# Small operations of two layer normalisations on GpSimd instead of VectorE and ScalarE, in a two-layer graph kernel

## The reference

```python
# layer 0
h = max(layernorm(x), 0)
x = x + (A @ (h @ W0 + b0)) / deg[:, None]        # A = adj != 0, deg = column sums of A
# layer 1: attention with 4 heads of 512 columns
h = max(layernorm(x), 0)
ht = (h @ W1) by head; src = ht . a_src; dst = ht . a_dst
e = leaky_relu(src[:, None] + dst[None, :], 0.01) + adj
x = x + mean over heads of softmax(e) @ ht
```

## Time and profile before

| | us |
|---|---|
| median of 3 runs | 2461.21 |
| the profiled execution's own time | 2460.44 |
| its span | 2458.6 |
| PE busy | 2434.6 |
| DVE busy | 1873.5 |
| ACT busy | 1269.3 |
| POOL busy | 47.9 |

### The profile page before, as it was taken

One profiled execution on the slowest core, in us unless ns is written; L12 is line 12 of the kernel. 1 busy time (PEld: TensorE's weight loads), 2 busy tenths in 40 slices (PEclk: granted clock), 3 DMA queues, 4 the chain that ended last, 5 costly groups with the idle time before them and its releaser, 6 DMA issues.

```text
span 2458.6 us, 43025 instructions
## 1 busy us (share of the span) xinstructions
PE 2434.6 (99%) x12447; PEld 1182.6 (48%) x12447; DVE 1873.5 (76%) x2580; ACT 1269.3 (52%) x1886; POOL 47.9 (2%) x44
## 2 busy tenths in 40 slices
PE   7999999999999999999999999999999999999999
PEld 4444445444444444444444444444444444444787
DVE  7788787977778667886668866688766887767786
ACT  5645558644455444554445544455444554454554
POOL 0000000000000000000000000000000000000000
PEclk9999999999999999999999999999999999999999
DMA  4386756100221001210012100121001300001000
GB/s 150 105 269 187 257 185 227 35 2 3 60 64 39 0 5 51 73 39 0 5 43 81 39 0 5 38 86 35 4 5 34 90 34 3 2 13 49 27 1 10
DMA packets 74225, 144.76 MB, mean 59 GB/s; under 512 B 4489, under 2 KB 11915, under 8 KB 72970
## 3 DMA queue, kind: packets, MB, share of 16 engines
q1 hardware_dynamic: 74122, 143.61, 18.3%
HBM read 129.11 MB, written 13.70 MB: 58 GB/s over the span
## 4 chain that ended last, share of the span: by engine, by line
PE 82%; DVE 0%; ACT 0%; issue 0%; DVEq 0%; ACTq 0%
PE z_ps L798 71%; PE o_ps L826 11%; PE c_ps L812 0%; DVE t_reg L685 0%; DVE e_reg L496 0%; ACT t_reg L581 0%; DVE hl_reg L657 0%; ACT hl_reg L596 0%; DVE ao_reg L729 0%; ACT ring_reg L1568 0%; DVE z_reg L701 0%; ACT z_reg L608 0%; ACT ao_reg L1563 0%; DVE vv L1357 0%; DVE ao_reg L672 0%
## 5 line engine op out<-in xcount | busy, mean ns | idle before, releaser
L798 PE MATMUL z_ps<-hl_reg,h_reg 128*128 (+2 forms) x8712 | 1752.0, 364 | 1.3 <-DVE hl_reg L657 1.3
L798 PEld LDWEIGHTS z_ps<-hl_reg,h_reg 128*128 (+1 forms) x8712 | 852.4, 98 | 897.5 <-issue 2.3
L596 ACT ACTIVATE hl_reg<-t_reg (+2 forms) x363 | 360.7, 994 | 722.7 <-DVE t_reg L685 379.4
L657 DVE TENSOR_TENSOR hl_reg<-t_reg,hl_reg (+2 forms) x363 | 416.1, 1146 | 229.9 <-ACT hl_reg L596 228.0
L581 ACT ACTIVATE t_reg<-ring_reg,vv 128x512 f32 (+3 forms) x726 | 524.8, 770 | 66.0 <-DVE ao_reg L672 60.1
L685 DVE SCALAR_TENSOR_TENSOR t_reg<-t_reg,vv,e_reg (+3 forms) x728 | 509.9, 741 | 7.9 <-issue 7.9
L672 DVE TENSOR_TENSOR ao_reg<-ao_reg,t_reg 128x1024 f32<-128x1024 f32 (+1 forms) x336 | 383.4, 1141 | 0.0
L826 PE MATMUL o_ps<-w_reg,z_reg 128*128 128x512 f16 x1248 | 278.2, 379 | 0.9 <-DVE z_reg L701 0.9
L701 DVE SCALAR_TENSOR_TENSOR z_reg<-z_ps,z_reg 128x512 f16<-128x512 f32 (+1 forms) x112 | 73.1, 653 | 151.6 <-ACT z_reg L608 151.6
L826 PEld LDWEIGHTS o_ps<-w_reg,z_reg 128*128 128x128 f16 x1248 | 119.8, 98 | 140.9 <-DVE z_reg L701 1.2
L485 ACT ACTIVATE e_reg<-e_reg (+2 forms) x91 | 90.5, 995 | 152.5 <-DVE e_reg L496 152.5
(11 more groups left out here) (203 smaller groups left out, 1071.8 us busy)
## 6 DMA issues: line engine op xcount, KB each, us to landing
ring_reg<-adjT_in SPq DMA_DIRECT2D x78, 512.0 KB, 4.7
e_reg<-adjT_in SPq DMA_DIRECT2D x78, 512.0 KB, 3.7
ao_reg<-x_dram SPq DMA_DIRECT2D x6, 1024.0 KB, 5.5
out_dram<-ao_reg SPq DMA_DIRECT2D x6, 1024.0 KB, 4.6
ring_reg<-c_dram SPq DMA_DIRECT2D x23, 256.0 KB, 3.4
h_reg<-x_in SPq DMA_DIRECT2D x3, 1536.0 KB, 16.5
ring_reg<-x_in SPq DMA_DIRECT2D x9, 512.0 KB, 4.2
x_dram<-ring_reg SPq DMA_DIRECT2D x9, 512.0 KB, 5.1
```

The source lines that it names most:

```text
L596: nc.scalar.activation(hl_ring[:, g % HL_RING, 0, :, 0:W], t_ring[:, g % T_RING, :, 0:W], ACT.Copy).then_inc(hi_ready, 1)
L657: nc.vector.tensor_tensor(hl_ring[:, g % HL_RING, 1, :, 0:W], t_ring[:, g % T_RING, :, 0:W], hl_ring[:, g % HL_RING, 0, :, 0:W], ALU.subtr ...
L798: mm = nc.tensor.matmul(z_ps[:, k, 0:W], hk[hs], hl_ring[:, r, ps, u, 0:W], start=first and u == 0 and n == 0, stop=last and u == 1 and n ...
```

## The change

- Layer 0's tiles are grouped in nine groups instead of six: (0,2), (2,4), (4,6), (6,8), (8,10), (10,12), (12,16), (16,20), (20,26). The first tile of x comes in a transfer of its own, then the second; W0's tiles and b0 are loaded ahead of tiles 2 and 3.
- The square root (ACT) and the five scalar operations (DVE) go, for both normalisations. POOL makes `rs` and `nb` by eight operations: variance plus eps, the power minus one half, a Newton step in four, and the negated mean and the bias. POOL's first reduction L1001 now stands after layer 0's nine groups, and layer 1's nine groups stand between L1003 and L1005.
- PE issues `wake_clock` matmuls in the opening (60, 10, 16, 8, of 128 columns), multiplies tiles 0 and 1 by weight tile in the order in which the splits come, and uses four PSUM banks for projected tiles. DVE and ACT take their opening work in a new order.
- `MAX_DVE` is two steps earlier.
- `exp_e(0, 1)` on ACT moves behind `t1(0, 0, 0)`.
- At the end, the last head's product waits for `z_lo` tile by tile; the last tile is made, added and stored by halves of 256 columns, the 15-row part from ACT's queue.

The core of the diff:

```diff
         def ln_variances(dve, t0, t1, written, n_written, count):
             dve.wait_ge(written, n_written)
             for t in range(t0, t1):
                 nc.vector.bn_aggr(mv3[:, t], bst3[:, t]).then_inc(count, 1)
-            dve.wait_ge(count, n_count)
-            nc.vector.tensor_scalar(ve[:, t0:t1], mv3[:, t0:t1, 1], EPS, None, ALU.add).then_inc(s_var, 1)

+        def ln_scalars(pool, t0, t1, count, n_count):
+            c = slice(t0, t1)
+            pool.wait_ge(count, n_count)
+            pool_link(pool, nc.gpsimd.tensor_scalar(ve[:, c], mv3[:, c, 1], EPS, None, ALU.add))
+            pool_link(pool, nc.gpsimd.tensor_tensor(y0[:, c], ve[:, c], mhalf[:, c], ALU.pow))
+            pool_link(pool, nc.gpsimd.tensor_tensor(y1[:, c], y0[:, c], y0[:, c], ALU.mult))
+            pool_link(pool, nc.gpsimd.tensor_tensor(y1[:, c], y1[:, c], ve[:, c], ALU.mult))
+            pool_link(pool, nc.gpsimd.tensor_scalar(y1[:, c], y1[:, c], -0.5 * HS, 1.5 * HS, ALU.mult, ALU.add))
+            nc.gpsimd.tensor_scalar(ve[:, c], mv3[:, c, 0], -1.0, None, ALU.mult).then_inc(pool_step, 1)
+            pool_steps[0] += 1
+            pool_link(pool, nc.gpsimd.tensor_tensor(rs[:, c], y1[:, c], y0[:, c], ALU.mult))
+            nc.gpsimd.tensor_tensor(nb[:, c], ve[:, c], rs[:, c], ALU.mult).then_inc(s_ln, 1)
...
-        MAX_DVE = MAX_PE + A_RING + A_MORE + 2
+        MAX_DVE = MAX_PE + A_RING + A_MORE
...
             t1(0, 0, 0)
+            exp_e(act, 0, 1)
...
+                    if final:
+                        for c in range(it + 1):
+                            cols = slice(c * D // (it + 1), (c + 1) * D // (it + 1))
+                            for k in range(KT):
+                                if it == 0:
+                                    pe.wait_ge(z_lo, q * KT + k + 1)
+                                for m, (zs, ws) in enumerate(((0, 0), (0, 1), (1, 0))):
+                                    mm = nc.tensor.matmul(o_ps[:, it + c, cols], z16[:, zs, k, it * P:(it + 1) * P],
...
                 pool.wait_ge(s_const, 6)
+                pool_link(pool, nc.gpsimd.memset(mhalf[:], -0.5))
+                for t0, t1 in groups0:
+                    ln_scalars(pool, t0, t1, s_mv, t1)
                 nc.gpsimd.partition_all_reduce(warm[:], ones32[:], P, RMAX).then_inc(s_lib, 1)
                 pool.wait_ge(s_wmx, 2)
                 nc.gpsimd.partition_all_reduce(wmax[:], wmx1[:], P, RMAX).then_inc(s_wmax, 1)
+                pool.wait_ge(h0_relu, NT)
+                for c, (t0, t1) in enumerate(groups1):
+                    ln_scalars(pool, t0, t1, s_mv1, tiles_of(c + 1))
                 pool.wait_ge(s_dmx, 1)
                 nc.gpsimd.partition_all_reduce(dall[:], dmx[:], P, RMAX).then_inc(s_dall, 1)
...
+                def first_products():
+                    for k in range(KT):
+                        pe.wait_ge(s_w0hi, k + 1)
+                        for t in range(2):
+                            pe.wait_ge(ht_hi, t + 1)
+                            nc.tensor.matmul(hid_bank(t), ht0[:, t, 0, k], w0_16[:, 0, k], start=k == 0, stop=False)
+                    for t in range(2):
+                        pe.wait_ge(ht_lo, t + 1)
+                        for k in range(KT):
+                            nc.tensor.matmul(hid_bank(t), ht0[:, t, 1, k], w0_16[:, 0, k], start=False, stop=False)
+                    for k in range(KT):
+                        pe.wait_ge(s_w0lo, k + 1)
+                        for t in range(2):
+                            nc.tensor.matmul(hid_bank(t), ht0[:, t, 0, k], w0_16[:, 1, k], start=False, stop=False)
+
+                def wake_clock(n):
+                    for i in range(n):
+                        nc.tensor.matmul(z_ps[:, 1, 0:P], b0_one, b0_one, start=True, stop=True)

                 pe.wait_ge(s_const, 6)
+                wake_clock(60)
                 transpose0(0)
                 transpose0(1)
+                wake_clock(10)
                 pe.wait_ge(s_w0mx, 1)
                 nc.tensor.matmul(z_ps[:, 0, 0:1], ones_m, w0mx[:], start=True, stop=True).then_inc(w0b_ps, 1)
-                hidden(0)
+                wake_clock(16)
+                first_products()
                 transpose0(2)
-                hidden(1)
                 transpose0(3)
+                pe.wait_ge(s_b0lo, 1)
+                hidden_bias(0)
+                hidden_bias(1)
+                wake_clock(8)
+                hidden(2)
+                hidden(3)
+                transpose0(4)
+                transpose0(5)
```

More of the change, by code:

```diff
@@ L228, in ln_variances @@
                 nc.vector.bn_aggr(mv3[:, t], bst3[:, t]).then_inc(count, 1)
-            dve.wait_ge(count, n_count)
-            nc.vector.tensor_scalar(ve[:, t0:t1], mv3[:, t0:t1, 1], EPS, None, ALU.add).then_inc(s_var, 1)
-        def ln_scalars(dve, t0, t1, group):
+        def ln_scalars(pool, t0, t1, count, n_count):
             c = slice(t0, t1)
[L235 to L247, removed]
+            pool.wait_ge(count, n_count)
[5 more added lines that the diff above has]
+            nc.gpsimd.tensor_scalar(ve[:, c], mv3[:, c, 0], -1.0, None, ALU.mult).then_inc(pool_step, 1)
+            pool_steps[0] += 1
+            pool_link(pool, nc.gpsimd.tensor_tensor(rs[:, c], y1[:, c], y0[:, c], ALU.mult))
+            nc.gpsimd.tensor_tensor(nb[:, c], ve[:, c], rs[:, c], ALU.mult).then_inc(s_ln, 1)
         order = [FULL] + list(range(FULL))
@@ L649, in layer2_scalar @@
             blocks(act, body, first=1)
+            r1 = FULL * BW + P
+            for c in range(2):
+                cols = slice(c * D // 2, (c + 1) * D // 2)
+                act.wait_ge(o_out, FULL * H * IT + H * LASTW // P + 2 + c)
+                nc.scalar.dma_start(out[r1 + LAST16:N, cols], out_acc[LAST16:LASTP, 1, cols]).then_inc(rest_st, 16)
+            act.wait_ge(rest_st, 32)
         def layer2_vector(dve, split1_one):
@@ L728, in add_out @@
                         dve.wait_ge(o_out, f - n + 3)
+                    if isinstance(b, int) and b == FULL and h == H - 1 and it == n - 1:
+                        for c in range(2):
+                            cols = slice(c * D // 2, (c + 1) * D // 2)
+                            dve.wait_ge(o_done, f + 2 + c)
+                            nc.vector.scalar_tensor_tensor(out=out_acc[:, it, cols], in0=o_ps[:, it + c, cols],
+                                                           scalar=rcoef[:, it:it + 1], in1=out_acc[:, it, cols],
+                                                           op0=ALU.mult, op1=ALU.add).then_inc(o_out, 1)
+                        continue
                     nc.vector.scalar_tensor_tensor(out=out_acc[:, it], in0=o_ps[:, it % 3],
@@ L819, in project @@
                 q = b * H + h
-                pe.wait_ge(z_lo, (q + 1) * KT)
+                final = isinstance(b, int) and b == FULL and h == H - 1
+                if not final:
+                    pe.wait_ge(z_lo, (q + 1) * KT)
                 for it in range(n):
                     pe.wait_ge(o_out, o_before(b, h) + 2 + (it >= 3))
+                    if final:
[6 more added lines that the diff above has]
+                                    mm = nc.tensor.matmul(o_ps[:, it + c, cols], z16[:, zs, k, it * P:(it + 1) * P],
+                                                          w16[:, k, h, ws, cols], start=k == 0 and m == 0,
+                                                          stop=k == KT - 1 and m == 2)
+                            mm.then_inc(o_done, 1)
+                        if it == 0:
+                            row_sums(b, h)
+                        continue
                     for k in range(KT):
@@ L1136, in hidden_sum @@
                     h = hid32[:, t % 3]
-                    ins = nc.vector.scalar_tensor_tensor(out=h, in0=o_ps[:, 2] if t % 2 == 0 else c_ps[:], scalar=SH,
+                    ins = nc.vector.scalar_tensor_tensor(out=h, in0=hid_bank(t), scalar=SH,
                                                          in1=b0_bc, op0=ALU.mult, op1=ALU.add)
@@ L1183, in _ @@
                 transposed_lo(1)
-                for k in range(KT):
+                stats0(2)
+                stats0(3)
+                variances0(1)
+                w0_lo(0)
+                for k in range(1, KT):
                     w0_lo(k)
                 b0_lo()
+                transposed_lo(2)
+                stats0(4)
+                transposed_lo(3)
+                stats0(5)
+                variances0(2)
+                hidden_lo(0)
+                stats0(6)
+                hidden_lo(1)
+                stats0(7)
+                variances0(3)
+                transposed_lo(4)
+                transposed_lo(5)
                 dve.wait_ge(s_const, 6)
-                for i in range(2, NT + 6):
-                    if 2 <= i - 2 < NT:
+                for i in range(6, NT + 6):
+                    if 6 <= i - 2 < NT:
                         transposed_lo(i - 2)
```

(2 more changed lines are left out.)

143 lines of the change are left out of this document (67 added, 76 removed).

## The result

The changed kernel takes **2466.82 us** (median of 16 runs, 2465.97 to 2467.45) against 2461.20 for the kernel before on the same chip (2460.15 to 2463.80): ratio 1.0021, 95% interval 1.0015 to 1.0027. The forecast was 2468.3, range 2457.5 to 2477.5. The profiled execution spans 2464.7 us; before it was 2458.6, so 6.1 us are to be found. Hidden(4) is the projection of tile 4 (`hidden`), a link one of the eight small operations with the wait behind it, and the chain all eight.

What follows compares the result with a forecast made beforehand. PE is busy 99%; only the opening, the passage from layer 1 to layer 2 and the tail are latency-bound. Terms -1.3 - 1.1 + 4.6 + 6.0 + 1.0 + 0.3 - 1.6 = +7.9 on 2460.44: 2468.3 us, range 2457.5 to 2477.5.

Steps and rivals of the forecast that it cites:

- Chain: Eight dependent GpSimd operations per normalisation group: 2.7 us undisturbed, bounds 1.5 and 5.5, longer beside two-input DVE operations.
- Rival 3: The power is slow in software: free chain 4.5 us, contended 6, total 2481.8 us; chance 0.12.
- Opening: Start of the kernel: first tile lands earlier, hidden(4) starts sooner despite a contended second chain; -1.3 us, bounds -4.3 and +4.
- rows_mx: Mid-kernel: early maxima reduced two steps earlier, so PE's 1.1 us wait for the row maxima goes; -1.1 us.
- Layer 1's loop: Layer 1's normalisation, groups 2 to 4: contended chains delay each turn, 3 x 2.0 less 1.4 slack; +4.6 us, bounds 0 and 10.
- Reduction: After layer 1's last group: GpSimd's change of kind, taken as 8.3 us, delays the reduction over dmx; +6.0 us, bounds +4.7, +9.
- Clock: Passage to layer 2: PE idles longer, so filler matmuls and layer 2's start may run at lower clock; +1.0 us.
- exp_e: Start of layer 2: exp_e(0, 1) moved behind t1 makes the first copy wait; +0.3 us, bounds -0.4 to +1.0.
- Tail: End of layer 2: z_lo wait goes, last addition by halves, stores on two queues; -1.6 us, bounds -0.8, -2.2.
- Rival 1: The lock costs little: no new layer 1 wait, opening -3.3, code switch +5.2; 2460.9 us, no change; chance 0.31.
- rival 2: Faster: GpSimd fetches the reduction's code while waiting or keeps both kinds, so only the chain precedes dall; 2454.3 us; chance 0.09.

Runs made afterwards that it cites:

- earlier_group: The changed kernel with layer 1's small operations back on DVE and ACT, plus layer 0's last group (tiles 20 to 25) one step earlier: 2455.52 us.
- ln1_on_dve: The changed kernel with layer 1's small operations back on DVE and its square root on ACT, layer 0's staying on GpSimd: 2456.56 us.
- before_ln1_pool: The kernel before with only layer 1's small operations moved to GpSimd, nothing else of the change: 2471.07 us.
- last_on_dve: The changed kernel with only layer 1's last group (tile 25) back on DVE and ACT: 2465.27 us.

## Why the prediction was right

The direction, the size (+6.1 against +7.9) and the mechanism came out: a chain that DVE's operations lengthen, paid in a loop, and a change of kind ahead of the reduction. The sizes of the two large terms did not. The terms, one by one:

- **Chain.** Taken as 2.7, with 0.28 a link and 0.7 for the power; measured 2.7, 0.27 and 0.74. (The upper bound was added up wrongly: eight times 0.47, seven times 0.11 and 1.27 are 5.8, not 5.5. Nothing hangs on it.) Rival 3 (a slow power) is out. What the bounds didn't foresee is that the power grows with the columns: 0.57 for one, 1.04 for four, 1.35 for six.
- **Opening.** -1.3 forecast, -2.18 measured. The contended chain was right (4.7 forecast, 4.4 measured), but the first statistics began 1.1 earlier (3.64, was 4.77 in the earlier trace rows), not 0.45. Then 1.0 was lost again where I had put nothing: the six-column group at 72 us was late (the waits of 0.35 and 0.55 at 77 us), and earlier_group got it back. That -1.17 reached mid-kernel, near the forecast, is luck.
- **rows_mx.** -1.1 forecast, -1.3 measured (from -1.17 to -2.48), but by two causes; and 0.65 more came from the last evacuation, which I had not counted.
- **Layer 1's loop.** +4.6 forecast, +7.28 measured, the term that was most off. The step was "3 x 2.0 - 1.4". The chain takes 4.56 from the last variance to the relu (358.83 to 363.39), 2.3 more than the 2.24 of the earlier trace rows, near the 2.0. But of the slack of 1.4 only 0.7 was left: these variances came 2.47 earlier than in the kernel before, PE 3.13 earlier, since the group ahead has a chain of its own and had already held DVE up. (With layer 1 on DVE, in ln1_on_dve, both come 2.3 earlier.) I had read the slack in one row of a kernel in which nothing was late. And a fourth group, of two tiles, wasn't in the sum. With nothing to wait for, PE's scores start 0.86 behind the start of the four matmuls ahead of them. At 365.17 it is 2.53 (1.67 lost), and the next scores lose 0.33. Counted like this the four groups cost 2.00, 2.19, 1.87 and 1.18, together 7.24 of the 7.28.
- **Reduction.** +6.0 forecast, +3.48 measured, below my lower bound of +4.7. The switch took 6.03 where I had 8.3, and 7.6 to 10 as its bounds. They came from a switch back to a tensor operation (7.58) and from the first reduction of the program (9.99, in the opening), and neither is the price of this one. In the 13 kernels traced, a switch back to a tensor operation costs 6.81 to 7.58; one towards a reduction costs 5.52 to 6.12, but for the program's first instruction of that kind behind the constants (9.99, and 10.02 in before_ln1_pool). The about 6 us of the Trainium skill (GPSIMD Engine Reference, "Instruction dispatch") fits the second, and the 3.6 worked out from it hits the measured 3.5; it does not hold for the first.
- **Clock.** +1.0 forecast, nothing measured. The nine fillers behind the last scores did run at the lower level (3.55 us instead of 2.10, granted clock 0.62 from 423.0 to 427.5), behind a wait of PE of 2.0, but they stand where PE waits for dall anyway, and the eleven of the next batch took 2.54, as before.
- **exp_e.** +0.3 forecast; the first product of layer 2 lost 0.26 on dall, and 0.1 was left by the third. No run moves exp_e alone, so that this 0.26 is its cost is not shown.
- **Tail.** -1.6 forecast, -1.65 measured, +1.7 when undone.

The sum of the parts, -3.13 + 7.28 + 3.48 + 0.1 - 1.65, is the +6.1. The misses of the two large terms, +2.7 and -2.5, cancelled: the total was closer than the parts deserve. Rival 1 had its opening no nearer than I did (-3.3, measured -2.18) and its lock wrong; rival 2 needed POOL to be ready for the reduction while it waits, which it is (last_on_dve), but only where the reduction is next in its queue.

That the price is layer 1's chain and what stands ahead of the reduction is shown by taking it out (ln1_on_dve) and by putting it alone into the kernel before (before_ln1_pool). That long links come from what DVE does is shown by the rows and by the two kernels with a one-input operation; which property of the DVE operation counts is only half shown. The Trainium skill (SBUF — State Buffer, "SBUF: two separate sides") has an exclusive lock that a vector operation takes with two SBUF inputs, and also in a two-port performance mode. The trace agrees for GpSimd's waits, down to operations of 0.2 us; whether the one-input operations that hold a link up run in such a mode no run here shows. It does not agree the other way round: by that section DVE would be blocked behind a GpSimd operation that started first, and the additions beside the power took their usual 1.41.

## What to carry to other kernels

Moving eight tiny operations to an idle engine made PE wait 7 us, because the chain stood in a loop whose every turn needs it: price such a move by the length of the chain where it will run (here 4.5 beside DVE, some 3.1 by the free links, 2.24 before), times the turns of the loop. Look at what else stands in the target engine's queue: the first instruction of another kind, put right behind a late one, showed 6 us of switch, and moving the last small group away hid all of it, at the price of a table load on ACT. In layer 0 the same operations cost PE less: 0.7 beside the splits of W0, and 1.0 for the group of six tiles, which an earlier start of that group took away. No kernel has layer 0's operations alone back on DVE and ACT, so what GpSimd gives or costs there is not shown. A change can be good in one place and bad in the next, and the two are worth testing apart.

## What was not expected of the hardware

- The power on GpSimd takes 0.57, 0.74, 1.04 and 1.35 us for 1, 2, 4 and 6 columns of 128 partitions, about 0.16 a column, while a multiplication stays at 0.19 to 0.23.
- GpSimd's switch between kinds has a direction: 5.52 to 6.12 us towards a partition reduction, 6.81 to 7.58 towards a tensor operation behind one.
- A GpSimd operation of 0.2 us that starts inside a DVE operation with two SBUF inputs, or inside a one-input conversion from one SBUF tile to another, is held up, mostly until that operation is over, and takes up to 1.23; beside statistics, reductions and operations that read PSUM it keeps its length. DVE's own operations aren't longer beside it.
- One square root on ACT between other functions cost 1.28 us of table load in the chain, and another 1.28 ahead of the exponential behind it, which stood off the chain (last_on_dve).
